# The low half of ctx: two subtractions moved from GpSimd to VectorE in each pass of a Flamingo block

## The reference

```python
# attention over ctx, on the layer-normed x
t = Wt @ ctx;  p = Wp @ layernorm(x);  g = Wg @ ctx        # 256x256 @ 256x1024
att = sum over each of 8 groups of p * g
y = blockdiag(Wz) @ (att * t)
yn = group_norm(y) * gn_w + gn_b + ctx
x = x + tanh(g_xattn) * yn
# low-rank mixture of experts, on the layer-normed x
h = layernorm(x)
gate = softmax over the top 16 of 64 scores (h @ Wq.T @ keys.T)
z = (h @ A_w.T) * gate              # 512 columns, 8 for each expert
x = x + tanh(g_ffn) * 2 * (z @ B_w.T)
```

## Time and profile before

| | |
|---|---|
| median of 3 runs | 394.64 us (394.6 to 395.23) |
| span of the profiled execution, first to last instruction | 392.9 us |
| time that lies around the span, taken as the median less the span | 1.7 us |
| PE busy | 367.8 us, 94% of the span |
| DVE busy | 293.8 us, 75% |
| ACT busy | 131.0 us, 33% |
| POOL busy | 96.8 us, 25% |
| mean granted TensorE clock | 0.991 of full speed |
| one pass | 44.92 us (from one hT(1) to the next: 54.17 to 323.71 us for six) |

### The profile page before, as it was taken

One profiled execution on the slowest core, in us unless ns is written; L12 is line 12 of the kernel. 1 busy time (PEld: TensorE's weight loads), 2 busy tenths in 40 slices (PEclk: granted clock), 3 DMA queues, 4 the chain that ended last, 5 costly groups with the idle time before them and its releaser, 6 DMA issues.

```text
span 392.9 us, 5668 instructions
## 1 busy us (share of the span) xinstructions
PE 367.8 (94%) x2051; PEld 321.2 (82%) x2051; DVE 293.8 (75%) x729; ACT 131.0 (33%) x204; POOL 96.8 (25%) x73
## 2 busy tenths in 40 slices
PE   6998489999999989999899989999899989999996
PEld 5776479888898878888798878988798878988994
DVE  3867899459974899649985799739985699738742
ACT  4574435203542136113432036213342035321310
POOL 0172152205140152304240150402440150401000
PEclk9999789999999999999999999999999999999999
DMA  7648001401150020501141011501132011001102
GB/s 257 237 139 300 15 2 44 172 0 54 53 214 0 12 95 6 207 0 53 53 160 54 0 53 53 214 0 53 53 100 113 0 53 53 0 0 53 55 24 84
DMA packets 10665, 30.36 MB, mean 77 GB/s; under 512 B 1937, under 2 KB 2705, under 8 KB 10657
## 3 DMA queue, kind: packets, MB, share of 16 engines
q1 hardware_dynamic: 10544, 30.19, 20.5%
q10 hardware_dynamic: 112, 0.07, 0.1%
HBM read 21.86 MB, written 8.39 MB: 77 GB/s over the span
## 4 chain that ended last, share of the span: by engine, by line
PE 77%; DVE 7%; POOL 6%; ACT 4%; issue 2%; DMA 2%; SPq 1%; ACTq 0%; POOLq 0%; DVEq 0%
PE w_ps L829 32%; PE z_ps L884 19%; PE w_ps L905 18%; DVE ln_sb L651 5%; POOL c_lo L294 4%; PE t_ps L870 4%; DMA x_sb<-in_x 2%; ACT c_hi L366 2%; PE t_ps L895 2%; PE w_ps L884 2%; POOL w_rs L316 1%; ACT hT_hi L396 1%; PE t_ps L812 1%; DVE x_st L501 1%; ACT q_hi L371 0%
## 5 line engine op out<-in xcount | busy, mean ns | idle before, releaser
L884 PE MATMUL z_ps<-A_hi,hT_hi 128*128 128x288 f32 x240 | 53.4, 304 | 0.6 <-DVE hT_lo L557 0.6
L884 PE MATMUL z_ps<-A_hi,hT_lo 128*128 128x288 f32 x240 | 51.9, 298 | 0.0
L884 PE MATMUL z_ps<-A_lo,hT_hi 128*128 128x288 f32 x240 | 51.9, 298 | 0.0
L905 PE MATMUL w_ps<-B_hi,zT_hi 128*128 128x512 f32 x128 | 51.3, 400 | 0.0
L304 POOL TENSOR_TENSOR q_lo<-ln_sb,q_hi 128x1024 fp32r<-128x1024 f32 x16 | 38.1, 2404 | 53.5 <-ACT q_hi L371 53.5
L905 PE MATMUL w_ps<-B_lo,zT_hi 128*128 128x512 f32 x128 | 49.9, 390 | 0.0
L905 PE MATMUL w_ps<-B_hi,zT_lo 128*128 128x512 f32 x128 | 49.9, 390 | 0.0
L396 ACT ACTIVATE hT_hi<-t_ps 128x512 fp32r<-128x512 f32 x32 | 17.4, 591 | 78.0 <-PE t_ps L870 78.0
L884 PEld LDWEIGHTS z_ps<-A_hi,hT_hi 128*128 128x128 f32 x240 | 39.4, 192 | 1.6 <-DVE hT_lo L557 1.0
L294 POOL TENSOR_TENSOR c_lo<-c_sb,c_hi 128x1024 fp32r<-128x1024 f32 x14 | 33.3, 2381 | 28.9 <-ACT c_hi L366 28.9
L884 PEld LDWEIGHTS z_ps<-A_lo,hT_hi 128*128 128x128 f32 x240 | 39.2, 192 | 0.0
(11 more groups left out here) (131 smaller groups left out, 787.8 us busy)
## 6 DMA issues: line engine op xcount, KB each, us to landing
x_sb<-in_x SPq DMA_DIRECT2D x8, 1024.0 KB, 5.0
c_sb<-in_ctx SPq DMA_DIRECT2D x7, 1024.0 KB, 7.0
out_block<-o_sb SPq DMA_DIRECT2D x14, 512.0 KB, 2.6
res_sb<-in_L_ffn_B_w SPq DMA_DIRECT2D x3, 512.0 KB, 3.5
c_sb<-in_ctx SPq DMA_DIRECT2D x2, 512.0 KB, 5.9
stage<-in_L_ffn_A_w SPq DMA_DIRECT2D x2, 512.0 KB, 6.3
res_sb<-in_L_ffn_A_w SPq DMA_DIRECT2D x2, 512.0 KB, 9.9
out_block<-o_sb SPq DMA_DIRECT2D x4, 256.0 KB, 2.0
```

The lines of the kernel that those rows point to most:

```text
L884: last = pe.matmul(banks[i][:, 0:ZH], h[:, t, row], w[:, k, i * ZH:(i + 1) * ZH], start=(k == 0 and h is hT_hi and w is A_hi), stop=(k == ...
L905: last = pe.matmul(w_ps[k][:, :], z[:, t, row], w[:, j, cols], start=(j == 0 and z is zT_hi and w is B_hi), stop=(j == KN - 1 and z is zT_lo))
```

## The change

POOL's ctx_low and its two calls are taken out. DVE gets a function of the same name, without the second wait (on the last product with the old c_lo; c_hi_s already comes after it), and calls it twice at the start of each pass. In the same place x_stats moves from ahead of hT_low(1) to behind it. The prologue uses the new function for what it did before.

```diff
@@ POOL
-            def ctx_low(t, n, prev):
-                pool.wait_ge(c_hi_s[t], n)
-                if t == 0:
-                    pool.wait_ge(p_done[USES - 1], prev)
-                return pool.tensor_tensor(c_lo[:, t, :], c_sb[:, t, :], c_hi[:, t, :].bitcast(f32), ALU.subtract)
...
             def next_attention(n, m):
-                ctx_low(0, m, n)
                 w_root(1, n)
-                ctx_low(1, m, n).then_inc(c_lo_s, 1)
                 x_root(m)
                 query_low(m)
                 y_root(m)
@@ DVE
+            def ctx_low(t, n):
+
+                dve.wait_ge(c_hi_s[t], n)
+                return dve.tensor_tensor(c_lo[:, t, :], c_sb[:, t, :], c_hi[:, t, :].bitcast(f32), ALU.subtract)
+
...
-            for t in range(T):
-                dve.wait_ge(c_hi_s[t], 1)
-                dve.tensor_tensor(c_lo[:, t, :], c_sb[:, t, :], c_hi[:, t, :].bitcast(f32), ALU.subtract)\
-                   .then_inc(c_lo_first if t == 0 else c_lo_s, 1)
+            ctx_low(0, 1).then_inc(c_lo_first, 1)
+            ctx_low(1, 1).then_inc(c_lo_s, 1)
             prep(n_first - 1)
...
             def ffn_and_next(n, m, n_dma, m_dma):
+                ctx_low(0, m)
+                ctx_low(1, m).then_inc(c_lo_s, 1)
+                hT_low(1, n)
                 x_stats(m, m_dma)
-                hT_low(1, n)
                 gate(0, n)
                 query(m, n)
                 x_plus_ctx(m, m_dma)
```

## The result

The changed kernel takes **409.84 us** (median of 4 runs, 406.64 to 410.13), the kernel before 394.62 us: ratio 1.036 (95% interval 1.032 to 1.039), so it is 15 us slower. The span of the profiled execution is 407.8 us (392.9 before), its time 409.61 us.

The account below looks back on a forecast made before the run. PE, 94% busy, bounds the kernel, so only its gaps can be won: 1.6 us before hT(1), less 0.6 before zT(0) and 0.2 for q_lo, is 0.8 a pass, 5.6 for seven: 389.0 us, range 386.5 to 400.5.

Parts of the forecast that it names:

- Steps 1 and 2: POOL loses both c_lo subtractions: DVE after h_tile(1) is 2.31 us earlier, and PE's 1.56 us gap before hT(1) closes.
- PE's first gap: PE's idle time before the transposes of hT(1), waiting for DVE's ln_sb: 1.56 us a pass, expected to close.
- Step 3: DVE does both c_lo subtractions after add_out(3), 2.37 us for the pair; PE's u products leave 1.7 us to spare.
- Steps 4 to 6: DVE runs hT_low(1), then x_stats: gate 0.59 us later, PE waits before zT(0), 1.0 us a pass left of 1.6.
- step 4: hT_low(1) ahead of x_stats: DVE waits 0.6 us for hT_hi, whose first half is done 0.59 us after its start.
- Step 7: DVE's query, x_plus_ctx and u_statistics end at 293.7, PE wants the group means at 294.2: 0.5 us to spare.
- Step 8: POOL's q_lo begins inside DVE's x_plus_ctx; DVE keeps the port through both instructions, POOL waits, PE loses about 0.2 us.
- the second rival: POOL's q_lo gets the port between x_plus_ctx's two instructions: 0.8 us a pass slower, about 400.2 us; chance 0.27.

Follow-up runs that it names:

- experiment 1: The changed kernel, with POOL's q_lo subtractions waiting until DVE has finished x_plus_ctx (xt_done); 390.26 us, ratio 0.988.
- experiment 5: The changed kernel, with two small POOL operations (128 x 2) between q_hi's signal and the first q_lo subtraction; 389.36 us, ratio 0.986.
- experiment 2: The changed kernel, with 8 products of 512 columns that nothing reads on PE ahead of the group means; 401.43 us, ratio 1.016.
- experiment 7: The kernel before, with only the second c_lo subtraction moved to DVE at the front of the pass, the first left on POOL; 383.92 us, ratio 0.972.
- experiment 8: The changed kernel, with 2 products of 512 columns that nothing reads on PE ahead of zT(0); 408.99 us, ratio 1.034.
- experiment 3: The changed kernel, with x_stats back ahead of hT_low(1), behind the two new subtractions on DVE; 399.49 us, ratio 1.012.
- experiment 4: The kernel before, with one added wait: POOL starts the second c_lo subtraction after h_tile(1) is done; 383.21 us, ratio 0.971.

## Why the prediction was wrong

- **Steps 1 and 2** (POOL gives w_rs and the port free, PE's first gap closes) held. All of h_tile's instructions are short now:

```profile
L648 DVE TENSOR_SCALAR ln_sb<-uw_sb,w_mv,w_rs x32: 536/542/547, 44.5 to 381.0; 128x512 f32<-128x512 f32 x32
```

- **Step 3** held: the pair of subtractions takes 2.35 us (2.37 forecast), and PE does not wait for c_lo.
- **Steps 4 to 6** held (the 0.59 of step 4, the first half of hT_hi, stands in none of the rows that it names, but the trace has it: 589 ns): DVE waits for hT_hi (0.53 us; 0.6 forecast), the gate is later, and PE's new gap before zT(0) is 0.58 us (0.6 forecast). From hT(1) to zT(0) PE has lost 0.70, and gained 1.6 before, so 0.9 a pass was won at this point (1.0 forecast).
- **Step 7**'s margin of 0.5 us for the group means was right, and it held in experiments 1 and 5 (0.46 us in the pass at 240 us of each).
- **Step 8 failed**, the overlap of x_plus_ctx and q_lo. It had q_lo's request in the right place (0.2 us before the end of the first x_plus_ctx instruction; forecast 0.19), and then took the case in which DVE keeps the port through both instructions. POOL got it between them, in all seven passes. This is the second rival, to which I gave 0.27, and its sizes were right too: the stop 2.15 us (2.05 to 2.3), the gap before the group means 1.66 us (just under the 1.7 to 1.9), and 0.9 us a pass in the passes without the low clock (0.8).
- **The price of that rival was too low.** It ended at 400.2 us, because no step asked what a new gap of 1.7 us does to PE's clock; the cost of the clock stands at nothing in every sum, and no reason is given. The kernel before, with a gap of 1.54 to 1.67 us in each pass and full clock, did not show it. The changed kernel shows 1.6 us more in five of seven passes, 8 us in all. With the clock kept up the same kernel takes 401.4 us (experiment 2), 1.2 us above the rival's time; the clock is what carried the result far out of the range.
- Where DVE does keep the port (experiments 1 and 5), the kernel takes 390.3 and 389.4 us, against the 389.0 forecast. The 1.3 us left in experiment 1 are mostly q_lo, for which PE waits 0.37 us a pass where I had 0.2. (The row at 296.78 that the prediction calls the first product with q_lo is one with q_hi, the first that waits for q_lo_s; the sum is not touched.)

The Trainium skill (SBUF — State Buffer, "SBUF: two separate sides") says that the pair of ports is held for the whole instruction by whoever starts first, and that a DVE operation with two SBUF inputs counts, against a GpSimd operation that reads SBUF. The changed kernel agrees (DVE held 2.15 us, then POOL about 1 us), and so do the first pass of experiment 2 and experiments 5 and 7, in which POOL is the one held (1.1, about 1 and 0.5 us).

Open: why the clock falls after the same gap in five of seven passes of the changed kernel, in six of seven in experiment 8 and in two of six in experiment 3, and in none of the profiled kernel before, whose gap is 1.54 to 1.56 us in six passes and 1.67 in the first, and stands in another place. No run varied the length or the place of the gap alone. The traces show this much: the fall has no fixed distance from the gap. It comes 0.5, 0.9, 1.2 and 1.5 us after the gap's end in four successive passes of the changed kernel, the pass after these has no fall, and the last has it at 0.3. In experiment 8 it comes after 1.1 and 1.5 us, then there is a pass without, then 0.3, 0.6, 0.9 and 1.2. The Trainium skill (TensorE: Matmul & The Clock Gate, "What's actually happening") says that the chip's check of activity runs freely and is not reset by the kernel; by that the same gap could fall well in one pass and badly in another. The moving distances fit this, but no run here moved the gap against that check to test it.

## What to carry to other kernels

When work leaves an engine, list every pair of instructions of DVE and POOL that both want SBUF, see from their durations which of them stop each other, and see whether the move brings two such together; a few tenths of a microsecond can decide, and the order of arrival should then be fixed by a semaphore and not left to chance. Look at what is queued behind the one that may be stopped before choosing who does the work: here one wait on POOL (experiment 4) gave 11.7 us, where moving the work cost 15. And give a new gap on a busy TensorE a second price, for the clock.

## What was not expected of the hardware

- After a gap of 1.66 us PE ran at full clock for 0.3 to 1.5 us and then at 1.2 GHz for a good 3 us, at 1.6 us of cost, in five of seven passes. With eight unread products in the gap it did not (experiment 2).
- A POOL operation of 128 x 2 elements takes 1.24 us if it starts just after a DVE instruction with two SBUF inputs; the same operation just ahead of it took 0.26 us (experiment 5).
- Between two DVE instructions that follow each other without a wait, POOL's request gets in: the second one was held 2.15 us though it was next in DVE's queue. POOL asked 0.1 us before it started; where POOL asked 0.03 us after (experiment 2, first pass), POOL was held.
- Not every DVE instruction is stopped: the four of u_statistics that run beside POOL's second q_lo (257.06 to 259.36 in the changed kernel) take 671 to 682 ns each, and all of this line 667 to 693 ns in the kernel before.
